# Projections over four PSUM banks, later queue entries, and split natural chunks kept in DRAM, in a cross-attention kernel

## The reference, cut to what matters

```python
qh = (q_in @ wq + bq).reshape(b, q_len, H, K)
kh = (kv_in @ wk + bk).reshape(b, t, H, K)
vh = (kv_in @ wv + bv).reshape(b, t, H, K)
kh = jnp.concatenate([kh, jnp.broadcast_to(bias_k, (b, 1, H, K))], axis=1)
vh = jnp.concatenate([vh, jnp.broadcast_to(bias_v, (b, 1, H, K))], axis=1)
logits = jnp.einsum('bqhk,bthk->bhqt', qh, kh) / scale
weights = jax.nn.softmax(logits, axis=-1)
ctx = jnp.einsum('bhqt,bthk->bqhk', weights, vh).reshape(b, q_len, H * K)
return ctx @ wo + bo
```

## Time and profile before

| | |
|---|---|
| median of 3 runs | 2390.76 us (2388.98 to 2396.07) |
| the profiled execution | 2392.78 us |
| its span, first to last instruction | 2391.0 us, mean granted TensorE clock 0.964 |
| TensorE busy | 2166.7 us, 91% of the span |
| VectorE, ScalarE, GpSimd busy | 1339.5, 1119.7, 842.3 us |
| DMA | 293.32 MB, mean 123 GB/s; main queue busy 46.2% of 16 engines' span |
| the twelve groups | 20 to 1731 us of the span |

### The profile page before, as it was taken

One profiled execution on the slowest core, in us unless ns is written; L12 is line 12 of the kernel. 1 busy time (PEld: TensorE's weight loads), 2 busy tenths in 40 slices (PEclk: granted clock), 3 DMA queues, 4 the chain that ended last, 5 costly groups with the idle time before them and its releaser, 6 DMA issues.

```text
span 2391.0 us, 34442 instructions
## 1 busy us (share of the span) xinstructions
PE 2166.7 (91%) x11876; PEld 2011.8 (84%) x11876; DVE 1339.5 (56%) x3230; ACT 1119.7 (47%) x2520; POOL 842.3 (35%) x770
## 2 busy tenths in 40 slices
PE   6989989888898988989898898989899989888999
PEld 4878889887888988888898888889899978877899
DVE  5636457464654745555475554637544567768441
ACT  4433345444334543344444343444455576657464
POOL 4133252432426224241523415143266611122255
PEclk8999999999999999999999999999999999999899
DMA  4744434365453434536343363633344466665233
GB/s 150 183 107 109 125 97 102 85 177 134 118 122 86 121 94 119 123 101 141 98 113 93 96 145 89 150 96 99 93 133 125 125 175 183 178 171 137 83 114 118
DMA packets 231410, 293.32 MB, mean 123 GB/s; under 512 B 112456, under 2 KB 157640, under 8 KB 231240
## 3 DMA queue, kind: packets, MB, share of 16 engines
q1 hardware_dynamic: 231240, 291.14, 46.2%
HBM read 258.84 MB, written 28.95 MB: 120 GB/s over the span
## 4 chain that ended last, share of the span: by engine, by line
PE 68%; DVE 9%; DMA 9%; ACT 9%; issue 4%; SPq 1%; POOL 1%; ACTq 0%; DVEq 0%; POOLq 0%
PE bank L1019 63%; DMA ctxN_raw<-in_ctx 5%; DVE QU L1718 2%; PE bank L1125 2%; ACT mring L1425 2%; ACT QU L1425 2%; DMA k<-k_parts 2%; DVE tmp L1848 1%; DMA stage<-in_wk 1%; PE bank L1091 1%; ACT prob L1541 1%; PE bank L1294 1%; DVE ctxT L1718 1%; DVE prob L1904 1%; DVE lnb L1760 1%
## 5 line engine op out<-in xcount | busy, mean ns | idle before, releaser
L931 POOL TENSOR_TENSOR mring<-stage,mring 128x512 fp32r<-128x512 f32 x389 | 522.5, 1348 | 397.6 <-ACT mring L1425 385.7
L1019 PE MATMUL bank<-pT,ctxN 128*128 128x500 f32 (+3 forms) x2304 | 494.5, 367 | 52.1 <-DVE ctxN L1718 33.3
L1019 PE MATMUL bank<-ctxT,QU 128*125 128x362 f32 (+1 forms) x2496 | 463.5, 337 | 37.3 <-DVE bank L1803 30.8
L1019 PEld LDWEIGHTS bank<-pT,ctxN 128*128 128x128 f32 (+1 forms) x2304 | 392.5, 200 | 103.8 <-DVE ctxN L1718 37.4
L1718 DVE TENSOR_TENSOR QU<-bank,QU 128x400 fp32r<-128x400 f32 (+2 forms) x512 | 280.8, 570 | 343.1 <-ACT QU L1425 342.7
L1019 PEld LDWEIGHTS bank<-ctxT,QU 128*125 128x125 f32 (+1 forms) x2496 | 425.5, 189 | 50.4 <-issue 35.7
L976 POOL TENSOR_TENSOR ctxN<-ctxN_raw,ctxN 128x384 fp32r<-128x384 f32 x144 | 145.5, 1021 | 583.6 <-ACT ctxN L1425 583.6
L1019 PE MATMUL bank<-hT,mring 128*128 128x400 f32 x1656 | 326.9, 349 | 10.9 <-ACT hT L1425 6.4
L1425 ACT ACTIVATE QU<-bank 128x400 fp32r<-128x400 f32 (+2 forms) x512 | 243.1, 497 | 187.7 <-PE bank L1019 185.7
L1019 PEld LDWEIGHTS bank<-hT,mring 128*128 128x128 f32 x1656 | 305.0, 190 | 20.0 <-issue 7.1
L1425 ACT ACTIVATE pT<-bank 128x375 fp32r<-128x375 f32 (+2 forms) x336 | 152.2, 453 | 239.4 <-PE bank L1125 214.8
(11 more groups left out here) (110 smaller groups left out, 2737.0 us busy)
## 6 DMA issues: line engine op xcount, KB each, us to landing
ctxT<-c_parts SPq DMA_DIRECT2D x96, 724.0 KB, 5.6
ctxN_raw<-in_ctx SPq DMA_DIRECT2D x192, 192.0 KB, 4.4
k<-k_parts SPq DMA_DIRECT2D x96, 181.0 KB, 3.6
stage<-in_wq SPq DMA_DIRECT2D x64, 256.0 KB, 2.5
stage<-in_wk SPq DMA_DIRECT2D x64, 256.0 KB, 2.6
stage<-in_wv SPq DMA_DIRECT2D x64, 256.0 KB, 2.6
stage<-in_wo SPq DMA_DIRECT2D x64, 256.0 KB, 2.6
stage<-in_fa SPq DMA_DIRECT2D x64, 256.0 KB, 2.6
```

Source lines behind the costliest of these rows:

```text
L931: nc.gpsimd.tensor_tensor(lo, src, f32(hi), ALU.subtract).then_inc(S.w_ready, 1)
L1019: mm = pe.matmul(dst, parts_l[a], parts_r[b], start=first and k == 0, stop=last and k == len(order) - 1)
```

## The change

- Queries, values and folds rotate over four banks (0 to 3); the extra logits use bank 4, and so wait for the last transposed tile of the group before, and the first output projection waits until they are copied out. The first two tiles of the whole kernel no longer wait for their extra logits; these are put in after the logits.
- Where a six-head group follows a five-head one, the last output projection comes after the last fold. `extra_add` and the first two `put_extra` of a group stand ahead of the four adds of the projected output to x. `value_low` follows at once where no fold comes next.
- `normalise` scales the whole row first and then copies column 0.
- The spread of a batch's probabilities is issued one batch later, the last one's in the next group's projections; the context for the second batch of the next group (turned) is issued four steps ahead of the group's end instead of at the last tile.
- Natural chunks are split in groups 0 and 3 alone and saved to DRAM in both parts (`n_parts`, 384 KB each, 32 saves); the ten other groups load both parts straight into `ctxN` (160 loads of 384 KB instead of 192 KB). A slot whose chunk is saved is loaded anew only when the save has landed.

```diff
@@ -137,8 +137,10 @@
             items.append(("k", G, s))
-        if s < before:
+        if s < before and (s < before - 1 or now <= before):
             items.append(("o", G - 1, s))
+    if now > before > 0:
+        items.append(("o", G - 1, before - 1))
     return items
@@ -271,6 +273,7 @@
     e_dram = nc.dram_tensor("e_rows", [NG, 2, NB * BROWS], F32, kind="Internal").ap()
+    n_dram = nc.dram_tensor("n_parts", [BATCH, DC, P, 2, PW], F32, kind="Internal").ap()
     q_dram = nc.dram_tensor("q_parts", [BATCH, P, 2, 4, LQ], F32, kind="Internal").ap()
@@ -343,7 +346,7 @@
         bank = [ctx.enter_context(nc.psum_tensor(f"bank{i}", [P, 512], F32)) for i in range(8)]
-        M_BANK, N_BANK, E_BANK = 5, 0, 3
+        M_BANK, N_BANK, E_BANK = 5, 0, 4
         T_BANK = [4, 5]
@@ -460,6 +463,7 @@
         S.ctx_saved = [sem(f"ctx_saved{k}") for k in range(2)]
+        S.ctxN_saved = [sem(f"ctxN_saved{k}") for k in range(DC)]
         S.ctxN_in = [sem(f"ctxN_in{k}") for k in range(DC)]
@@ -538,7 +542,7 @@
         def proj_bank(key):
-            return bank[PROJ_AT[key] % 3][:, 0:ROWS]
+            return bank[PROJ_AT[key] % 4][:, 0:ROWS]
@@ -702,8 +706,24 @@
                     sp.wait_ge(S.u_mm, last_unit(G - 1, NB - 1, c))
-                sp.dma_start(ctxN_raw[:, c, 1, :], T["ctx"][stage_of(G)[0] * NB + b, :, c * PW:(c + 1) * PW])\
-                    .then_inc(S.ctxN_in[c], 16)
+                before = NB * G + b - 1
+                if before in SAVED:
+                    sp.wait_ge(S.ctxN_saved[c], 16 * (SAVED.index(before) + 1))
+                batch = stage_of(G)[0] * NB + b
+                if G in RAW_GROUPS:
+                    sp.dma_start(ctxN_raw[:, c, 1, :], T["ctx"][batch, :, c * PW:(c + 1) * PW])\
+                        .then_inc(S.ctxN_in[c], 16)
+                else:
+                    sp.wait_ge(S.ctxN_saved[c], 16 * (batch + 1))
+                    sp.dma_start(f32(ctxN[:, c]), n_dram[batch, c]).then_inc(S.ctxN_in[c], 16)
+
+            def save_ctxN(G, b, c):
+                g = RAW_GROUPS.index(G)
+                if b < NB - 1:
+                    sp.wait_ge(S.cN_lo, DC * (NB - 1) * g + DC * b + c + 1)
+                else:
+                    sp.wait_ge(S.cN_last, DC * g + c + 1)
+                sp.dma_start(n_dram[stage_of(G)[0] * NB + b, c], f32(ctxN[:, c])).then_inc(S.ctxN_saved[c], 16)
@@ -825,8 +845,12 @@
             for G in range(NG + 1):
+                if G == NG:
+                    spread_p0(G - 1, NB - 1)
                 for j in range(FIRST_JOB[G], FIRST_JOB[G + 1]):
                     load_jobs(j + 1 + MS + STAGE)
+                    if 0 < G < NG and j - FIRST_JOB[G] == 2:
+                        spread_p0(G - 1, NB - 1)
                     if G < NG and j - FIRST_JOB[G] == heads(G) + 1:
@@ -842,16 +866,20 @@
                     if i < NB * n and i % n == n - 1:
-                        load_ctxT(NB * G + i // n + 2)
-                    if i < NB * n and i % n == n - 1:
+                        if i // n < NB - 1:
+                            load_ctxT(NB * G + i // n + 2)
                         save_p0(G, i // n)
-                    if i >= 2 and i - 2 < NB * n and (i - 2) % n == n - 1:
-                        spread_p0(G, (i - 2) // n)
+                        if i // n > 0:
+                            spread_p0(G, i // n - 1)
                     for b, c, k in sums_at(G, i):
+                        if G in RAW_GROUPS:
+                            save_ctxN(G, b, c)
                         if k == passes(G) - 1 and b < NB - 1:
...
                             load_ctxN(G + 1, 0, c)
+                    if i == group_steps(G) - 4:
+                        load_ctxT(NB * G + NB + 1)
             for F in range(NF):
@@ -972,7 +1000,7 @@
             def natural_low(G, b, c):
-                pool.wait_ge(S.cN_hi, 16 * G + DC * b + c + 1)
+                pool.wait_ge(S.cN_hi, 16 * RAW_GROUPS.index(G) + DC * b + c + 1)
                 nc.gpsimd.tensor_tensor(ctxN[:, c, 1, :], ctxN_raw[:, c, 1, :], f32(ctxN[:, c, 0, :]), ALU.subtract)\
@@ -984,10 +1012,11 @@
                 for c in range(DC):
-                    natural_low(G, 0, c)
+                    if G in RAW_GROUPS:
+                        natural_low(G, 0, c)
                 for i in range(group_steps(G)):
                     for b, c in naturals_at(G, i):
-                        if b < NB - 1:
+                        if b < NB - 1 and G in RAW_GROUPS:
                             natural_low(G, b, c)
@@ -1053,8 +1082,8 @@
                 n = PROJ_AT[key]
-                if n >= 3:
-                    pe.wait_ge(S.proj_done, n - 2)
+                if n >= 4:
+                    pe.wait_ge(S.proj_done, n - 3)
@@ -1087,6 +1116,8 @@
                 pe.wait_ge(S.proj_done, PROJ_AT["q", G, h, 0] + 1)
+                if h == 0 and G:
+                    pe.wait_ge(S.pt_lo, last_tile(G - 1))
                 for p_ in range(2):
@@ -1106,7 +1137,8 @@
                         pe.wait_ge(S.proj_done, proj_after(G))
-                pe.wait_ge(S.e_put, n + 1)
+                if n >= 2:
+                    pe.wait_ge(S.e_put, n + 1)
                 first, last = tile_columns(G, b, j)
@@ -1132,10 +1164,12 @@
                 if k == 0:
-                    if b < NB - 1:
-                        pe.wait_ge(S.cN_lo, DC * (NB - 1) * G + DC * b + c + 1)
+                    if G not in RAW_GROUPS:
+                        pe.wait_ge(S.ctxN_in[c], 16 * (NB * G + b + 1))
+                    elif b < NB - 1:
+                        pe.wait_ge(S.cN_lo, DC * (NB - 1) * RAW_GROUPS.index(G) + DC * b + c + 1)
                     else:
-                        pe.wait_ge(S.cN_last, DC * G + c + 1)
+                        pe.wait_ge(S.cN_last, DC * RAW_GROUPS.index(G) + c + 1)
                 if un >= 2:
@@ -1166,6 +1200,8 @@
                     pe.wait_ge(S.pt_lo, last_tile(G))
+                    if G < NG - 1:
+                        pe.wait_ge(S.e_copied, G + 2)
                 for c in range(DC):
@@ -1601,7 +1637,7 @@
                     k = j - FIRST_JOB[G]
-                    if G < NG and k in (5, 6, 7, 8):
+                    if G in RAW_GROUPS and k in (5, 6, 7, 8):
                         natural_high(G, 0, k - 5)
@@ -1618,7 +1654,8 @@
                     for b, c in naturals_at(G, i):
-                        natural_high(G, b, c)
+                        if G in RAW_GROUPS:
+                            natural_high(G, b, c)
                     if G in LN_GROUP and i == 13:
@@ -1796,7 +1833,9 @@
                 dve.wait_ge(S.e_ready, G + 1)
-                if at < 2:
+                if n < 2:
+                    dve.wait_ge(S.s_mm, n + 1)
+                elif at < 2:
                     dve.wait_ge(S.proj_mm, proj_after(G))
@@ -1819,13 +1858,12 @@
                 at = n - TILE[G, 0, 0]
+                nc.vector.tensor_scalar(x, x, rden[0:size, k:k + 1], None, ALU.mult).then_inc(S.p_ready, 1)
                 if b == 0 and j == 0 and G:
...
                         dve.wait_ge(S.p0_out[k_], 16 * G)
-                nc.vector.tensor_scalar(p0_col[0:size, at:at + 1], x[:, 0:1], rden[0:size, k:k + 1], None, ALU.mult)\
-                    .then_inc(S.p0_copied, 1)
-                dve.wait_ge(S.p0_copied, n + 1)
-                nc.vector.tensor_scalar(x, x, rden[0:size, k:k + 1], None, ALU.mult).then_inc(S.p_ready, 1)
+                dve.wait_ge(S.p_ready, n + 1)
+                nc.vector.tensor_copy(p0_col[0:size, at:at + 1], x[:, 0:1]).then_inc(S.p0_copied, 1)
@@ -1947,7 +1985,7 @@
             def natural_low(G, b, c):
-                dve.wait_ge(S.cN_hi, 16 * G + DC * b + c + 1)
+                dve.wait_ge(S.cN_hi, 16 * RAW_GROUPS.index(G) + DC * b + c + 1)
                 rest(ctxN[:, c, 1, :], ctxN_raw[:, c, 1, :], ctxN[:, c, 0, :]).then_inc(S.cN_last, 1)
@@ -1991,8 +2029,17 @@
                         value_low(*late)
-                    late = (g, h) if kind == "v" else None
+                        late = None
+                    if kind == "v":
+                        if PROJ[G][PROJ[G].index((kind, g, h)) + 1][0] == "k":
+                            late = (g, h)
+                        else:
+                            value_low(g, h)
                     if (kind, h) == ("o", heads(G - 1) - 1):
+                        if G < NG:
+                            extra_add(G)
+                            put_extra(TILE[G, 0, 0])
+                            put_extra(TILE[G, 0, 0] + 1)
                         for c in range(DC):
@@ -2002,12 +2049,14 @@
                 first, n = TILE[G, 0, 0], NB * tiles_of(G)
-                extra_add(G)
-                put_extra(first)
-                put_extra(first + 1)
+                if G == 0:
+                    extra_add(G)
+                    put_extra(first)
                 for i in range(group_steps(G)):
...
                         maximum(first + i)
+                    if G == 0 and i == 0:
```

(3 more changed lines are left out.)

## The result

The kernel after takes 2283.43 us (median of 4 runs, 2280.58 to 2286.36). In the same series the kernel before took 2393.41 us (2388.98 to 2396.11). The ratio is 0.9542, interval 0.9521 to 0.9564: 110 us less, where 130 were forecast. The profiled execution took 2283.64 us, with a span of 2281.9.

What follows compares the result with a forecast made beforehand. TensorE, busy 91% of the span, was taken as the bound, its stalls also slowing its clock. Terms 64 + 28 + 3.5 + 37.5 + 21 - 24 = 130 us saved gave 2260.8 us; range 2228 to 2306.

Steps and rivals of the forecast that it cites:

- Fold: Projection rounds of the head groups: a fourth bank removes the wait before each head's fourth fold, 64 us (bounds 30 and 75).
- rival 3: Projection rounds: the next values wait for the first fold's bank instead, 50 of 64 us lost, 2311 us; chance 0.06.
- rival 1: Fold of the keys: weights become the bound, leaving 2.5 to 3 us more per group, 2291 us; chance 0.17.
- Start: First logits of the eleven later groups: earlier puts and a later last output save 28 us (bounds 20 and 32).
- Group 0: Start of the first group: two tiles of logits run before the extra logits are there, saving 3.5 us.
- Five-head ends: Ends of six non-splitting five-head groups: chunk stall goes, 25 us, and following matmuls speed up, 12.5 us; together 37.5.
- Six-head ends: Last batch of the four six-head groups: ScalarE's chunk stall, slow clock and part of a tile wait go, 21 us.
- Splitting groups: Groups 0 and 3: added saves and reloads in SP's queue cost 12 us a group, 24 in all (bounds 0 and 50).
- TensorE has two steps in hand: Middle of groups 0 and 3: ScalarE may wait 7 us for a chunk, costing TensorE 0 to 6 us, taken as 3.
- Rival 2: Groups 0 and 3: saves hide, so their 24 us do not arise, and the clock stays up; 2231 us; chance 0.12.
- Rival 4: Tiles of five-head groups: natural chunks bind the DMA engines, slower than before, 2421 or 2500 us; chance 0.03.
- Rival 5: Whole kernel: the change does nothing measurable, as the four adds and the waits move into its place; chance 0.02.

## Why the prediction was right, and where it was not

In the phases above, the slow first logits of five groups (7.8 us of lost clock) lie in the tiles, while the wait ahead of them lies in the projections; below they are put back to the start.

**Fold.** The mechanism is right, the size low. The round was to last 6.54 us and lasts 6.56. The forecast was 64 us with bounds 30 and 75; run alone it is 70, taken away 75. By the phases: the nine groups that follow no splitting one gained 534.2 - 454.7 = 79.5 us, and G1 and G4 would bring 112.2 - 2 x 47.0 = 18.2 if they came down to the 47.0 us of G7. Of these 97.7 us 23.5 are the waits of the starts, so 74.2 are left. ScalarE's late weight and its half-hidden wait came as told (2.37 and 1.10 us; 8.6 us in all where 8 were taken off), and so did the 0.6 us in the groups after a six-head one (0.57 to 0.83). So the 10 us too few lie in none of the terms taken off. TensorE idles 56 us less inside these phases; the other 18 are shorter gaps and faster matmuls, for which I had 47 x 0.2 = 9.4. That term was mis-sized, and no row splits it further. The values wait at the bank that rival 3 named, but only once in seven of the eleven groups and behind the late weight, 8.6 us and not 50; rival 1's 2.5 to 3 us in every group didn't come either. Both are out.

**Start.** Right. The wait for the put fell from 30.8 to 3.9 us, all of it in group 0, and the first logits of all later groups run at full clock: 23.5 + 7.8 = 31.3 us in eleven groups, where I gave 28. The put's place is confirmed by its own run, for 17 us of the wait.

**Group 0.** The forecast gave it 3.5 us of gain at its start, and the wait for the put there did fall from 7.3 to 3.9. Its projections are shorter (30.4 for 38.2 us) since this wait stood at their end, but the tiles are 17.4 us longer: in all it is 9.6 longer.

**Five-head ends.** The step that failed is "I take 5", the landing of a pair chunk, drawn from the medians of the earlier trace rows. Over the kernel the median is 5.1 us, so the figure was right as a median, but the chunk that ends the stall is the one behind the save of probabilities, and takes 8.25 us (9.80 on another chip). I moved the context out of its way and left the other transfer unweighed, though SP's queue held it ahead of this chunk in the kernel before as well:

```profile
984.79 0.28 SPq L712 DMA_DIRECT2D p_rows<-p_col  x1
```

"So the stall goes" was wrong by 14 of 25 us: 2.1 to 2.7 us stay at each of the six ends. The gain was 464.3 - 439.5 = 24.8 us, of which 3 are the start's clock: 21.8, not 37.5.

**Six-head ends.** 389.6 - 359.7 = 29.9 us, less 4.8 of the start's clock: 25.1, not 21. The last 1.35 us of wait for a transposed tile stay, near the 1.1 us that the forecast left.

**Splitting groups.** The one large miss. Forecast 24 us, bounds 0 to 50. Measured: group 0 is 9.6 longer, where 3.5 of gain were forecast, so 13.1; the projections of G1 and G4 are 7.2 and 9.3 longer than the 47.0 us of their like, and the tiles of G3 18.5 longer than before: 48 us. Where the loss would stand was right: saves in the chain, SP late with the first weights. What it would cost was not. The first step to fail is "I take 4.3" for every save. The median is 4.2, but in group 3 those behind a context or a save of probabilities take 5.7 to 10.3 us, and they are the ones that others wait for. The second is the overlap "TensorE has two steps in hand", at 3 us a group: ScalarE splits the turned context in its turn behind the late chunks, and TensorE waits for it, 8.9 us in the middle of G3 where it was 3.3. The third is the end of the group, "where the stall stays (no gain)": TensorE idles 10.8 us there in place of 4.4. These two make 12 of G3's 18.5 us; the rest is matmuls at a lower clock, 0.81 against 0.97. And at the next group's first weight ScalarE waits 9.9 us, not "about 7". By the Trainium skill, "DMA: Bandwidth & Descriptors", section "Anatomy of one DMA", a DMA costs 2.0 us plus its bytes at 436 GB/s, an estimate of 2.9 us for a save of 384 KB. The page fits this for DMAs that GpSimd issues, and these are issued by SP, which the prediction doesn't say. The shortest saves of this trace agree with it (3.0 to 3.2 us). As the price of every save it would have led me further off, since it holds no queue.

**Sum.** The errors in us: fold +10.2, start +3.3, six-head ends +4.1, five-head ends -15.7, splitting groups and the 3.5 us of group 0 -24.1. That makes -22, as the phases have it (107.8 against 130); by the medians it is -20. The measured 2283.4 us lies in the range (2228 to 2306), but above my own forecast of 2240 to 2280, and in part by luck: gains put 40 us too high met gains put 18 us too low. The upper end of the range came from rival 1, which did not occur, and one more term at its lower bound, not from the saves. Rival 2 (the saves hide) is out: without them groups 0 and 3 and the projections behind are 50 us shorter. Rival 4 (chunks bind) didn't occur: the DMA share in the tiles of G6 (905 to 947 us) is 0.76 at 181 GB/s, against the 0.84 worked out. Rival 5 is out by the result.

My tests said that I'd be wrong if ordinary ends still wait for a chunk, or if groups 0 and 3 lose over 25 us each. The first occurred, the second for group 3 (27.8 with G4's projections) and not for group 0 (20.3 with G1's).

## What to carry to other kernels

A median landing time prices a transfer that nobody waits for. For one on the critical path, look at what stands directly ahead of it in its queue, small transfers too (here the save of 2 KB counted, and the spread of 250 KB did not), and put the transfer that an engine needs next ahead of them. Where a queue waits for its own saves, issue each save as soon as its data is ready; with the reloads moved behind the next weights, and at the same bytes, that was worth 52 to 65 us here. And if a change has several parts, undo each one alone: the largest in code, the saved chunks, brought nothing measurable as it stood.

## What the runs showed that I had not expected

The save of 2 KB: a chunk directly behind it lands in 9.51 us, one behind it and a spread in 8.25 to 9.80, and with neither ahead in under 6.6.

VectorE's instructions get longer beside GpSimd's. In the kernel before, a normalise of 125 x 362 took 1.23 us beside a GpSimd split that began 0.02 us later:

```profile
964.76 1.23 DVE L1828 TENSOR_SCALAR prob<-prob,stat 125x362 f32<-125x362 f32 x1
964.78 1.01 POOL L976 TENSOR_TENSOR ctxN<-ctxN_raw,ctxN 128x384 fp32r<-128x384 f32 x1 [1.76 <-ACT ctxN L1425]
```

The groups of this form have a mean of 662 ns before, 412 after, and 444 in the run where every group splits (line, form, count, then busy us and mean ns; after, then that run):

```profile
L1861 DVE TENSOR_SCALAR prob<-prob,stat 125x362 f32<-125x362 f32 x128 | 52.7, 412 | 4.5
```

```profile
L1852 DVE TENSOR_SCALAR prob<-prob,stat 125x362 f32<-125x362 f32 x128 | 56.8, 444 | 4.5
```

So the removed splits are not what made it shorter: with all of them in place it stays near 444 ns. With four banks alone it is 686. What is left is the small edit beside it, by which the normalise starts ahead of the copy of column 0 and can miss the split; it wasn't run alone. By the Trainium skill, "SBUF — State Buffer", section "Who interferes with whom", the two engines share a pair of ports, and where both need it the one that issues first blocks the other for its whole instruction. The lengths would fit that, 1.23 us being more than GpSimd's whole 1.01; the order doesn't, since the longer instruction is the one whose row begins 0.02 us earlier. Spans on GpSimd are rough, so the rows don't settle it. The other way round, the low part of the values went from 846 to 1425 ns in the mean (1422 with four banks alone). In the shorter round it meets the low part of a weight (timeline of the kernel after):

```profile
996.89 1.59 DVE L1751 SCALAR_TENSOR_TENSOR v_parts<-tmp,cols,v_parts 128x400 fp32r<-128x400 f32 x1
996.76 1.29 POOL L959 TENSOR_TENSOR mring<-stage,mring 128x512 fp32r<-128x512 f32 x1 [0.79 <-ACT mring L1461]
```

That both meetings decide the durations is read from the rows; no run took one away alone.

Last, the two chips that ran the kernel after differ at the ends and not in the rounds: the projections of G7 take 47.0 and 46.9 us, the tiles 72.3 and 74.9.
